# Second-layer attention by groups of four heads instead of pairs, in tiles of the TensorE array

## The reference

```python
x = x + _L0_attn_ref(_layernorm(x), ...)
x = x + _L0_ffn_ref(_layernorm(x), ...)
x = x + _L1_attn_ref(_layernorm(x), W_qkv, W_o)   # the attention that changes
x = x + _L1_ffn_ref(_layernorm(x), weight)
# in _L1_attn_ref, with q and k after the rotation:
scores = jnp.einsum('bhqd,bhkd->bhqk', q, k) / jnp.sqrt(jnp.float32(dk))
scores = jnp.where(causal[None, None, :, :], scores, -jnp.inf)
attn = jax.nn.softmax(scores, axis=-1)
out = jnp.einsum('bhqk,bhkd->bhqd', attn, v)
return jnp.einsum('bsd,ed->bse', out.transpose(0, 2, 1, 3).reshape(B, S, H * dk), W_o)
```

## Time and profile before

| what | value |
|---|---|
| median of 3 runs | 3582.85 us (3581.64 to 3582.94) |
| profiled execution, its own time | 3588.78 us |
| its span | 3586.9 us |
| TensorE / VectorE / ScalarE / GpSimd busy | 91 / 55 / 44 / 26% |
| granted TensorE clock, mean | 0.941 |

### The profile page before, as it was taken

One profiled execution on the slowest core, in us unless ns is written; L12 is line 12 of the kernel. 1 busy time (PEld: TensorE's weight loads), 2 busy tenths in 40 slices (PEclk: granted clock), 3 DMA queues, 4 the chain that ended last, 5 costly groups with the idle time before them and its releaser, 6 DMA issues.

```text
span 3586.9 us, 58807 instructions
## 1 busy us (share of the span) xinstructions
PE 3273.3 (91%) x20560; PEld 2333.5 (65%) x20560; DVE 1987.1 (55%) x6976; ACT 1567.3 (44%) x3441; POOL 927.5 (26%) x1840
## 2 busy tenths in 40 slices
PE   4999789998899979999899998999889998899978
PEld 3676657765677656776567765677656766567665
DVE  3664565555556465554656546566455554566445
ACT  1444344543454334543445525445253542544424
POOL 0222322222222222222222232222322223222222
PEclk7999899998999989999899998999999998999989
DMA  2000000000000000000000000000000000000000
GB/s 80 30 19 7 6 13 25 19 7 1 19 19 19 7 1 25 19 13 7 1 25 19 13 7 1 31 13 13 6 1 31 19 7 6 13 19 19 7 6 7
DMA packets 31438, 53.75 MB, mean 15 GB/s; under 512 B 3472, under 2 KB 13456, under 8 KB 30864
## 3 DMA queue, kind: packets, MB, share of 16 engines
q1 hardware_dynamic: 31120, 49.64, 4.3%
HBM read 44.91 MB, written 4.72 MB: 14 GB/s over the span
## 4 chain that ended last, share of the span: by engine, by line
PE 79%; DVE 11%; issue 4%; POOL 3%; ACT 2%; PEld 1%; PEldq 1%; SPq 0%; DMA 0%; POOLq 0%; ACTq 0%; DVEq 0%
PE outs L896 14%; PE work L820 7%; PE work L781 7%; PE work L857 6%; PE work L802 6%; PE work L858 5%; PE work L859 5%; PE work L903 4%; PE outs L1007 3%; DVE work L1124 3%; PE work L777 3%; PE work L786 2%; PE work L997 2%; PE work L861 2%; PE work L791 2%
## 5 line engine op out<-in xcount | busy, mean ns | idle before, releaser
L1480 ACT ACTIVATE PR<-work 128x512 f32<-128x512 f32 (+1 forms) x1088 | 640.5, 597 | 580.3 <-PE work L859 477.3
L1124 DVE CUSTOM_DVE_ANT_0 work<-work,KEEPB 128x384 f32<-128x384 f32 (+3 forms) x1536 | 665.5, 480 | 75.5 <-PE work L820 74.1
L1606 POOL TENSOR_SCALAR_AFFINE_SELECT PR<-PR 128x256 f32<-128x256 f32 (+1 forms) x960 | 348.3, 366 | 952.5 <-ACT PR L1480 948.6
L1108 DVE TENSOR_TENSOR BIG<-work,BIG 96x512 fp32r<-96x512 f32 (+1 forms) x455 | 285.4, 629 | 355.0 <-ACT BIG L1375 355.0
L820 PE MATMUL work<-BIG 96*128 96x448 f32 (+9 forms) x1664 | 447.9, 367 | 36.6 <-DVE NMX L1124 15.9
L1596 POOL TENSOR_TENSOR TOK<-AB 128x256 f32<-128x256 f32 (+1 forms) x325 | 219.2, 674 | 877.5 <-DVE AB L1078 854.8
L896 PE MATMUL outs<-PR,ONES 128*32 128x512 f32 (+4 forms) x2304 | 404.5, 458 | 0.0
L857 PE MATMUL work<-BIG 99*128 99x512 f32 (+4 forms) x1152 | 404.5, 351 | 0.0
L820 PEld LDWEIGHTS work<-BIG 96*128 96x128 f32 (+1 forms) x1664 | 285.2, 207 | 174.7 <-issue 91.7
L1077 DVE TENSOR_TENSOR AB<-work,COS 128x256 f32<-128x256 f32 (+2 forms) x357 | 150.0, 420 | 426.9 <-PE work L781 366.3
L858 PE MATMUL work<-BIG 96*128 96x512 f32 (+4 forms) x1152 | 382.4, 332 | 0.0
(11 more groups left out here) (161 smaller groups left out, 5280.9 us busy)
## 6 DMA issues: line engine op xcount, KB each, us to landing
WKW<-w_kw_dram SPq DMA_DIRECT2D x65, 256.0 KB, 2.8
WSEL<-w_sel_dram SPq DMA_DIRECT2D x65, 256.0 KB, 3.0
X<-x_dram SPq DMA_DIRECT2D x9, 512.0 KB, 3.4
out_dram<-X SPq DMA_DIRECT2D x9, 512.0 KB, 2.8
WFC<-w_fc_dram SPq DMA_DIRECT2D x1, 1024.0 KB, 9.9
WFP<-w_ffp_dram SPq DMA_DIRECT2D x1, 1024.0 KB, 11.9
WQKV<-w_qkv_dram SPq DMA_DIRECT2D x1, 768.0 KB, 13.0
WQ<-w_q_dram SPq DMA_DIRECT2D x1, 576.0 KB, 7.4
```

The lines of the kernel that those rows point to most:

```text
L1108: read_work(v.tensor_tensor(dst[1], src, dst[0].bitcast(F32), ALU.subtract), use)
L1124: last = v.tensor_tensor_reduce(ps[:, lo:hi], ps[:, lo:hi], KEEPB[:, T - (hi - lo):T], -1.0, -NEG, ALU.add, ALU.min, dst)
L1480: a.activation(PR[0:rows, j % NP, :], ps[0:rows, :], ACT.Exp).then_inc(exp_ready, 1)
L1606: gp.affine_select(blocks, blocks, [[0, len(cols)], [1, P]], ALU.is_ge, 0.0, base=0, channel_multiplier=-1).then_inc(exp_masked, 1)
```

## The change

Second-layer attention goes by groups of four heads (4 groups) instead of pairs (8). One step now issues two banks of scores for two heads whose operands lie in rows 0 to 63 and 64 to 127, product by product in turn. Values run in four column tiles for four heads. Queries are held once (QS), the maximum's row at row 32 of each head's 64; maxima of a group lie 32 columns apart in a new buffer NMX1, so that one set of transposes brings them to partitions 0, 32, 64 and 96. The due times are set anew. Masks and exponentials stay as many as they were.

```diff
-PV = [[(2 * k, 2 * k + 1) for k in range(6)], [(0, 1), (2, 3), (4,)]]
+NB = [NPAIR, NG]
+SPAN = [1, 2]
+PV = [[(2 * k, 2 * k + 1) for k in range(6)], [(0, 1, 2, 3), (4, 5, 6, 7), (8, 9)]]
...
-         dict(pv=3.09, tr=1.9, group=2.19, max=-0.3, max_gap=1.03, mt=2.68, pro=-0.08,
+         dict(pv=3.09, tr=1.9, group=2.19, max=-2.0, max_gap=0.8, mt=2.4, pro=-0.08,
...
-        b = n * (p - (1 if layer == 0 else 2))
+        b = n * (p - 1)
...
-        for i in range(len(MAX_UNITS[layer])):
+        for i in range(0, len(MAX_UNITS[layer]), span):
             at.append((b + o["max"] + o["max_gap"] * i, ("max", p, i)))
...
-            t = max(o["piece"] + o["gap"] * m + o["piece_tr"], n * (NPAIR - 1) - 0.9 + 0.01 * m)
-            at += [(o["piece"] + o["gap"] * m, ("piece", NPAIR, m)), (t, ("piece_tr", NPAIR, m))]
+            t = o["piece"] + o["gap"] * m
+            at += [(t, ("piece", NPAIR, m)), (t + o["piece_tr"], ("piece_tr", NPAIR, m))]
...
-        QZ = BIG[:, 0:8192].rearrange("p (g h k) -> p g h k", g=NPAIR, h=2)
-        KB = BIG[:, 8192:12288].rearrange("p (g k) -> p g k", g=NPAIR)
+        QS, KB = (BIG[:, 4608:12800].rearrange("p (g s k) -> p g s k", g=NPAIR, s=2)[:, :, n, :] for n in range(2))
...
+        NMX1 = sb("NMX1", [P, 2, 100])
...
+            def row_tiled(jobs):
+                for n in range(len(jobs[0][2])):
+                    for ps, done, products in jobs:
+                        cols, left, right = products[n]
+                        last = mm(ps[:, cols], left, right, start=(n == 0), stop=(n == len(products) - 1))
+                        if n == len(products) - 1:
+                            last.then_inc(done, 1)
+
+            def head_rows(h):
+                return slice(64 * (h % 2), 64 * (h % 2) + 64)
...
+                if layer == 1:
+                    jobs = []
+                    for u in (i, i + 1):
+                        ps, done = take((1, "max", p, u), W)
+                        jobs.append((ps, done, [(slice(col, col + n),
+                                                 QS[head_rows(h), 2 * p + h // 2, qt * P:(qt + 1) * P],
+                                                 KB[head_rows(h), 2 * p + h // 2, k0:k0 + n])
+                                                for h, _, k0, n, col, qt in MAX_UNITS[1][u]["mm"]]))
+                    return row_tiled(jobs)
...
-                        last = nc.tensor.transpose(ps[0:2, t * P:(t + 1) * P], NMX[:, p % 2, t:8:NT], ID[:, :])
+                        last = nc.tensor.transpose(ps[0:97, t * P:(t + 1) * P], NMX1[:, p % 2, t:t + 97], ID[:, :])
...
+                if layer == 1:
+                    jobs = []
+                    for u in (i, i + 1):
+                        ps, done = take((1, "unit", p, u), W)
+                        jobs.append((ps, done, [(slice(col, col + T - j * P),
+                                                 KB[head_rows(h), 2 * p + h // 2, j * P:(j + 1) * P],
+                                                 QS[head_rows(h), 2 * p + h // 2, j * P:T])
+                                                for _, h, j, col in UNITS[1][u]]))
+                    return row_tiled(jobs)
...
-                for n in range(0, len(parts), 2):
+                tiles = HG if layer else 2
+                for n in range(0, len(parts), tiles):
...
-                            row = 64 * (p % 2 if layer else side) + 32 * h
+                            row = 64 * side + 32 * h
...
-                        read_work(a.activation(QZ[2 * D1:2 * D1 + 2, p, h, :], ps[0:2, :], ACT.Copy,
-                                               scale=ID[0:2, h:h + 1]), (1, "mt", p))
+                    for h in range(HG):
+                        row = 64 * (h % 2) + 2 * D1
+                        read_work(copy(QS[row:row + 1, 2 * p + h // 2, :], ps[32 * h:32 * h + 1, :]), (1, "mt", p))
...
-                        for h in range(2):
-                            read_work(a.activation(QZ[:, 4 * n:4 * n + 4, h, t * P:(t + 1) * P],
-                                                   ps[:, :].rearrange("p (g k) -> p g k", g=4), ACT.Copy,
-                                                   scale=HEAD[:, h:h + 1]), ("heads", t, n))
+                        read_work(copy(QS[:, 4 * n:4 * n + 4, t * P:(t + 1) * P],
+                                       ps[:, :].rearrange("p (g k) -> p g k", g=4)), ("heads", t, n))
```

More of the change, by code:

```diff
@@ L171, in attention_steps @@
             for a in COMPLETE[layer].get(k, []):
[L172 to L177, removed]
+                group = layer == 1 or (a == A2 and p % 2)
                 t1 = t + 0.3 + o["tr"]
-                at += [(t + 0.3, ("out", what, a)), (t1, ("out_tr", what, a)), (t1 + 0.1, ("norm", what, a))]
+                at += [(t + 0.3, ("out", p, a)), (t1, ("out_tr", p, a)), (t1 + 0.1, ("norm", p, a))]
                 if layer == 0 and a == A2:
@@ L281, in attention @@
                     work.use((0,) + s + (h,))
-            elif s[0] in ("unit", "max", "mt", "out_tr", "group"):
-                work.use((layer,) + s, {"unit": 0, "mt": 2}.get(s[0], 1))
+            elif s[0] in ("unit", "max"):
+                for i in range(s[2], s[2] + SPAN[layer]):
+                    work.use((layer, s[0], s[1], i), int(s[0] == "max"))
+            elif s[0] in ("mt", "out_tr", "group"):
+                work.use((layer,) + s, HG if s[0] == "mt" else 1)
             elif s[0] in ("piece", "piece_tr"):
@@ new lines, in unit @@
+                ps, done = take((0, "unit", p, i), W)
+                for n_part, (a, h, j, col) in enumerate(UNITS[0][i]):
+                    q0, keys = j * P, (KEEP if a == A2 else P)
+                    out = ps[0:keys, col:col + T - q0]
+                    stop = n_part == len(UNITS[0][i]) - 1
+                    q = [QW[p % 2][n][:, h, q0:T] for n in range(2)]
+                    if a == A3:
+                        k = [QW[p % 2][n][:, 2 + h, j * P:(j + 1) * P] for n in range(2)]
+                    else:
+                        k0 = 0 if a == A2 else KEEP + j * P
+                        k = [K1[p % 2][n][:, h, k0:k0 + keys] for n in range(2)]
+                    mm(out, k[0][0:D0 + 3], q[0][0:D0 + 3], start=(col == 0), stop=False)
+                    mm(out, k[0][0:D0], q[1][0:D0], start=False, stop=False)
+                    last = mm(out, k[1][0:D0], q[0][0:D0], start=False, stop=stop)
@@ L1165, in attention @@
                     elif s[0] == "max":
-                        maxima(layer, s[1], s[2])
+                        for i in range(s[2], s[2] + SPAN[layer]):
+                            maxima(layer, s[1], i)
                     elif s[0] == "norm":
@@ L1490, in attention @@
                     elif s[0] == "unit":
-                        exponentials(layer, s[1], s[2])
+                        for i in range(s[2], s[2] + SPAN[layer]):
+                            exponentials(layer, s[1], i)
                     elif s[0] == "out":
```

93 lines of the change are left out of this document (37 added, 56 removed).

## The result

The changed kernel takes 3614.05 us (median of 4 runs, 3612.56 to 3617.28) against 3582.89 of the kernel before in the same series: ratio 1.0086, interval 1.0071 to 1.0101. It is 31 us slower; 36 us faster was forecast, and the range ended at 3583.

What follows compares the result with a forecast made beforehand. VectorE was taken to bound most of the second-layer stage, TensorE its tail. Start 0.9, maxima stretch 3.6 and tail 0 made 4.5 us a sequence, 36 in 8: 3582.85 to 3547 us, range 3507 to 3583.

Steps and rivals of the forecast that it cites:

- stretch from first to last maximum: Second-layer stage, VectorE's first to last maximum: forecast 44.9 us from 48.5, 3.6 us off a sequence.
- Start of stage: Query copies before the stage: two instead of four per row tile, so the stage starts 0.9 us earlier.
- VectorE's work unchanged, 40.0: First to last maximum: maxima, next sequence's prologue and two normalisations still take VectorE 40.0 us.
- Idle terms, 4.9: First to last maximum: new VectorE idle time from transposes, copies, prologue, half clock and bank waits, 4.9 us in total.
- TensorE waits for the four copies: At group 2, TensorE waits for the copies, then runs a value product before the next maxima: 0.9 us.
- Clock, 0.4: First to last maximum: half clock slows only the first transposes (1.01 against 0.60 us), 0.4 us.
- Rival C: TensorE waits between maxima steps and its clock falls to 1.2 GHz: 5.5 us a sequence slower, 3627; chance 0.11.
- from a little under half of the stretch at half clock: Share of the first-to-last-maximum stretch at half clock from which the clock rival decides (4.5 us lost).
- The tail, 22.3 to 22.3: Last maximum to last value product: 3.3 us of transposes and copies plus 19.0 of queued work; nothing gained.
- Values, scores: TensorE in one sequence: four heads' values cost what two do, 10 us off; scores in two row tiles, 5 off.
- one-by-one end of my bound: Score steps: if four weight loads go one by one, a step takes 0.42 us; 0.21 if they overlap.
- the 17 us a sequence that TensorE was to lose: TensorE's work in the stage: some 17 of its 73 us saved, not all of it a gain in time.

Runs made afterwards that it cites:

- e5: Changed kernel plus six useless 512-column products at each of four waits for the maxima copies in a sequence's second-layer stage; 3569.91 us.
- before: The kernel without the change, second-layer attention by pairs of heads; 3582.89 us.
- e3: Changed kernel with ScalarE copying one head's maxima per group instead of four, the other three left out of their scores; 3539.03 us.
- after: The changed kernel as described, measured against the kernel without the change; 3614.05 us, ratio 1.0086.
- e15: The kernel without the change, plus two extra 320-column ScalarE copies ahead of each pair's two, into a buffer nothing reads; 3615.91 us.
- e16: Changed kernel, maxima copies shared by ScalarE and VectorE except group 1's, all on ScalarE; copies due 0.05 behind the transposes; 3593.32 us.
- e10: Changed kernel, each group's four maxima copies shared by ScalarE and VectorE, plus six useless products in the copy waits; 3569.32 us.
- e17: As e16, plus three useless products in the copy waits; 3548.12 us.
- e9: Changed kernel with each group's four maxima copies shared, heads 0 and 2 on ScalarE, 1 and 3 on VectorE; 3577.00 us.

## Why the prediction was wrong

Two terms of the stretch from first to last maximum failed. VectorE's idle time was put at 4.9 us and measured 11.8, above all because the copies hold a bank of the ring; and the clock was put at 0.4 us where fillers alone (e5) give back 5.5 a sequence. From VectorE's first maximum (876.17) to its last the stretch takes 51.2 us, where 44.9 was forecast and before takes 48.5.

**Start of stage** (0.9 earlier): right in kind. The query copies are two a tile, and between stages 2.0 us a sequence are saved; what the second 1.1 is was not tested.

**VectorE's work unchanged, 40.0**: right, 39.6.

**Idle terms, 4.9**: the step that failed first. VectorE idles 51.9 - 39.6 = 12.3 us in the stretch as cut in the result, 11.8 of them from its first maximum on. With one copy it is 6.1 (45.24 - 39.12). The terms that I had read from the order stand at their places (1.99 at group 0's end for the 1.4 forecast; 1.47 at group 2's for 1.3, and at group 1 prologue steps do cover the transposes). What I sized at 0.9, "TensorE waits for the four copies", I had for group 2 alone. It comes at group 1 too, and it is longer (3.38 and 2.57): the transposes' bank comes round to the second next maxima step, and with it VectorE's maxima. I had counted the two banks of a step, not whose bank it would be next. With one copy the stretch is 45.2, what I had forecast for four.

**Clock, 0.4**: the second failure, of about equal size. I saw 0.57 in the row of before and priced it for transposes alone. e5 shows 5.5 us a sequence. Rival C named the mechanism. Its own 5.5 is another quantity, 10 us for a stretch wholly at half clock less the 4.5 that I expected to gain; that its 3627 lies near the 3614 measured is in part luck, since it had half of the loss, the copies' wait, at nothing. I gave it 0.11 because TensorE ran at 1.00 from 885 to 901 while also waiting for VectorE. But in that stretch it was busy for 13.05 of 16.00 us, where now it is for 3.92 of 9.00, 4.72 of 8.40 and 5.13 of 9.20, with waits of up to 3.4 us: the very work that the change saves, and the waits that it adds, are what the argument against C rested on. My own condition, "from a little under half of the stretch at half clock", was met: the clocks of the five stretches to 927.5, weighted by their spans, make 0.71, which is 0.59 of the time at half clock.

**The tail, 22.3 to 22.3**: 25.0. Transposes and copies take the 3.2 I had; what follows takes 21.6 for 19.0. e3, at a clock of 1.00 throughout, takes 20.1 there. So about 1.5 go with the clock, and 1.1 are left, switches or order that I under-priced; no run parts these.

**Values, scores**: right. Sixteen records of 384 and 128 columns take 1.07 us at full clock; two banks of scores for two heads 0.50. The Trainium skill ("TensorEngine Tiling (Array Packing)", Key Properties) says that different tiles can load weights and multiply in parallel; the 0.50 agrees. The four weight loads of such a step take 0.30 (after, 910.50), so the one-by-one end of my bound (0.42 a step and the pipeline's end) falls away. Of the 17 us a sequence that TensorE was to lose it lost 10 (66.81 busy before, 56.53 after), records at half speed among them, and in e3 14. None of it was worth anything until the waits and the clock were mended.

In sum for the second sequence: forecast 68.0 from first maxima product to W_o, measured 76.8. e3 gives 67.3, so the 9.5 above it come with the copies. e5, which leaves the copies and mends the clock, gives 71.96 in this sequence: by that 4.8 are the clock and 4.7 the waits. The split is an estimate, since e5 also leaves less half clock than e3 (17 us for 24). Each of the two costs time by itself: e5 changes only the clock, e15 only the copies, and within e16 the clock changes with no change in the instructions. But they don't add. In this kernel the clock falls behind the waits, and with both treated (e10) the gain is that of the fillers alone. What decides whether the clock returns in e16 stays open. So does the best cure: two due times, more banks in the ring, or fewer copies could do more than e17; they weren't tried.

## What to carry to other kernels

When a change takes work off TensorE in a stage where another engine sets the pace, price the clock first: read its granted clock beside its busy share, and ask which waits the change lengthens. A gain in TensorE's busy time can come back as a loss. Where buffers go round a ring in a fixed order, follow each buffer to its next user: a reader that is slow once holds up a step that has nothing to do with it. And a serial tail of small copies costs by their number and their columns; how many partitions each has made no difference here (0.60 us for 1 and for 128). Last, a trial of one order says little while the clock can fall differently in the next: read its granted clock too.

## What the hardware showed

- Useless products made the kernel faster: 192 of them, 44 us. "TensorE: Matmul & The Clock Gate" of the Trainium skill (section "A second HAM failure mode: psum-queue depth-cycling") tells of a TensorE that idles briefly between groups while cycling through banks, and loses by its clock. This case agrees: with waits of 1.4 to 3.4 us at the ring the second stage of after has a mean clock of 0.78, with fillers in them 0.88 (e5).
- One instruction stream on one core can have stages of 71.1 and 75.2 us in one execution (e16).
- A ScalarE copy of one partition and 512 columns takes 0.60 us (2.42 for four), as much as one of 128 partitions (`ACT NRM<-outs` of 128x512 in after, 0.60).
- ScalarE and VectorE read one PSUM bank at once, at different partitions, in 1.20 and 1.42 us for two copies each (e9). "PSUM — Partial Sum Buffer" of the Trainium skill counts a collision by bank and quadrant; partitions 0 and 64, 32 and 96 lie in different ones, and the trace shows no delay: two of VectorE's copies take the same 1.42 at group 1 (897.92), where most of their time has ScalarE done.
